# The opening of a second cross attention in a four-stage block: where the first queries, both query biases, the key blocks and two norms stand in their queues

## What is computed

```python
x = x + _L0_xattn_ref(_layernorm(x), ctx_768, ...)      # cross attention, 16 heads of 64
x = x + _L0_ffn_ref(_layernorm(x), ...)                 # shared MLP + top 2 of 8 experts
x = x + _L1_xattn_ref(_layernorm(x), ctx_768, ctx_768, ...)
x = x + _L1_ffn_ref(_layernorm(x), ...)                 # fp8 product with one scale over all of x
```

```python
Qp = query @ Wq + bq
K = _l2norm(key @ Wk + bk)
V = value @ Wv + bv
Q = _l2norm(Qp)
... # 16 heads of 16
scores = einsum('bhqd,bhkd->bhqk', Q, K) * SCALE
out = einsum('bhqk,bhkd->bhqd', softmax(scores), V)
x = out @ Wo + bo + Qp
... # then a layer norm with gamma and beta
```

## Time and profile before

| | |
|---|---|
| median of 3 runs | 931.23 us (927.85 to 932.57) |
| the profiled execution | 929.04 us, its span 927.0 us |
| PE busy | 859.7 us, 93% |
| PE weight load busy | 788.0 us, 85% |
| DVE busy | 723.2 us, 78% |
| ACT busy | 526.5 us, 57% |
| POOL busy | 361.9 us, 39% |
| mean granted TensorE clock | 0.961 of full speed |

### The profile page before, as it was taken

The page is one execution under the profiler, slowest core; times in us unless marked ns, Lnnn a source line. Parts: engine busy times, 40 slices in busy tenths (PEclk is TensorE's granted clock), DMA queues, the critical chain, the costliest instruction groups (busy, mean ns, idle before and its releaser), DMA issues. The chain is left out here.

```text
span 927.0 us, 18650 instructions
## 1 busy us (share of the span) xinstructions
PE 859.7 (93%) x5904; PEld 788.0 (85%) x5904; DVE 723.2 (78%) x1821; ACT 526.5 (57%) x1454; POOL 361.9 (39%) x412
## 2 busy tenths in 40 slices
PE   6899999999999999999979999999899999999435
PEld 6889999999999998899969999998688888888423
DVE  7788788978978978888756667877636889978988
ACT  5676566656756655454424445444436566665377
POOL 3133333423333424765631310243654757341330
PEclk9999999999999999999989999999879999999768
DMA  9999980000100003343324434544211111000003
GB/s 303 304 334 321 328 272 0 0 0 0 34 0 0 2 1 104 103 141 110 103 75 120 140 101 134 151 132 133 79 52 41 52 41 47 24 1 2 0 23 159
DMA packets 51771, 91.89 MB, mean 99 GB/s; under 512 B 5381, under 2 KB 26298, under 8 KB 51697
## 3 DMA queue, kind: packets, MB, share of 16 engines
q1 hardware_dynamic: 45105, 72.87, 24.7%
q0 software_dynamic: 6592, 18.07, 6.3%
HBM read 34.56 MB, written 56.36 MB: 98 GB/s over the span
## 5 line engine op out<-in xcount | busy, mean ns | idle before, releaser
L535 POOL TENSOR_TENSOR prob<-prob,row_inv 128x462 f32<-128x462 f32 (+1 forms) x96 | 83.6, 874 | 180.4 <-DVE row_inv L711 180.4
L898 PE MATMUL acc<-u,probT 128*128 128x256 f32 (+1 forms) x960 | 134.2, 289 | 1.0 <-DVE u L723 1.0
L595 ACT ACTIVATE prob<-score,neg_max 128x77 f32<-128x77 f32 x512 | 120.9, 351 | 14.6 <-DVE neg_max L705 14.3
L851 PE MATMUL score<-m,xnT 128*128 128x462 f32 (+1 forms) x576 | 124.2, 354 | 0.0
L898 PEld LDWEIGHTS acc<-u,probT 128*128 128x128 f32 (+1 forms) x960 | 119.5, 189 | 1.9 <-DVE u L723 1.4
L851 PEld LDWEIGHTS score<-m,xnT 128*128 128x128 f32 x576 | 97.6, 191 | 6.0
L1231 PE MATMUL py<-w1T,hidT 128*128 x426 | 93.5, 355 | 0.0
L2128 PEld LDWEIGHTS acc<-vz,prob 128*128 128x128 f32 (+1 forms) x640 | 80.2, 199 | 12.8 <-issue 11.2
L585 ACT ACTIVATE probT<-tr 128x512 fp32r<-128x512 f32 (+1 forms) x96 | 52.0, 544 | 66.3 <-PE tr L837 66.0
L1676 POOL DMA_INDIRECT dispatched<-xn,slots x64 | 69.2, 1082 | 43.9 <-DVEq L1460 26.6
L2128 PE MATMUL acc<-vz,prob 128*128 128x34 f32 (+2 forms) x640 | 82.4, 283 | 0.0
(11 more groups left out here) (381 smaller groups left out, 2086.7 us busy)
## 6 DMA issues: line engine op xcount, KB each, us to landing
dispatched<-zeros SPq DMA_DIRECT2D x1, 33664.0 KB, 111.0
xn<-dispatched SPq DMA_DIRECT2D x71, 128.0 KB, 2.0
dispatched<-hid SPq DMA_DIRECT2D x71, 128.0 KB, 1.7
out<-x_res SPq DMA_DIRECT2D x7, 512.0 KB, 2.6
x_res<-in_x SPq DMA_DIRECT2D x1, 3072.0 KB, 16.0
consts<-in_L_ffn_W SPq DMA_DIRECT2D x8, 384.0 KB, 3.4
consts<-in_L_ffn_Ws SPq DMA_DIRECT2D x3, 384.0 KB, 3.8
x_res<-in_x SPq DMA_DIRECT2D x2, 512.0 KB, 9.2
```

The lines of the kernel that those rows point to most:

```text
L535: gp.tensor_tensor(pr, pr, row_inv[t % 2][:, heads(k)].unsqueeze(2).to_broadcast([P, BANK_HEADS[k], KEYS]), ALU.mult).then_inc(prob_ready, 1)
L595: last = act.activation(prob[t % 2][:, h * KEYS:(h + 1) * KEYS], score_of(t, k)[:, n * KEYS:(n + 1) * KEYS], ACT.Exp, bias=neg_max[t % 2][ ...
L851: last = pe.matmul(score_of(t, k)[:, 0:BANK_HEADS[k] * KEYS], xnT[blk][i][:, dc, j * P:(j + 1) * P], m[w][:, dc, cols(k)], start=(n == 0 a ...
L898: last = pe.matmul(acc[t % 2][:, 0:D], probT[t % 2][i][0:rows, c, :], u[k][0:rows, c, :], start=(c == 0 and q == 0), stop=(c == KCH - 1 an ...
```

## The change

Four lists are written in another order; no instruction is added or taken away.

- PE and DVE: block 0's queries come behind two value rows instead of four, and DVE adds both biases one behind the other instead of with four value rows between them. The second half of the combine of block 1, its statistics, the low parts of block 0's queries and its shift are placed anew between the value rows. On PE two value rows (14 and 15) move behind the transposes of the queries.
- POOL: `gp_keys(0, 0)` comes behind the first gather of block 2, and `gp_ln(1)` behind two more gathers.
- ACT: the norm of block 1 stands in one piece behind the first two exponentials, where it had stood around them; the norm of block 2 comes before the copies of block 1's transposed queries, where it had stood behind them.

```diff
--- before.py
+++ after.py
@@ -2261,11 +2261,11 @@
             act_exp(act, 0, 8)
             act_unit_queries(act, 1)
             act_exp(act, 0, 9)
+            for a in range(2):
+                act_normalize(act, 2, a)
             act_split_q(act, 1, 0)
             act_turned(act, 0, 0)
             act_split_q(act, 1, 1)
-            for a in range(2):
-                act_normalize(act, 2, a)
             act_exp(act, 1, 0)
             act_exp(act, 1, 1)
             for dc in range(DC):
@@ -2602,13 +2602,14 @@
             @block.gpsimd
             def _(gp):
                 gp_gather(gp, 1, FIRST_PART)
-                gp_keys(gp, 0, 0)
                 for k in range(YT_BUFS):
                     gp.wait_ge(g["stored"][k], 16 * len(range(k, TILES_B, YT_BUFS)))
                 gp_gather(gp, 2, 0, 1)
+                gp_keys(gp, 0, 0)
                 gp_root(gp, 0)
+                gp_gather(gp, 2, 1, 3)
                 gp_ln(gp, 1)
-                gp_gather(gp, 2, 1, TJ)
+                gp_gather(gp, 2, 3, TJ)
                 gp_keys(gp, 0, 1)
                 gp_gather(gp, 2, TJ)
                 gp.memset(bias_rows[:, :], 0.0).then_inc(fs["rows_set"], 1)
@@ -2644,10 +2645,10 @@
                 act_unit_queries(act, 0)
                 for dc in range(DC):
                     act_split_q(act, 0, dc)
-                act_normalize(act, 1, 0)
                 act_exp(act, 0, 0)
                 act_exp(act, 0, 1)
-                act_normalize(act, 1, 1)
+                for a in range(2):
+                    act_normalize(act, 1, a)
                 act_first_block(act)
                 for n in range(1, NBLK):
                     act_block(act, n)
@@ -2714,17 +2715,18 @@
             def _(dve):
                 dve_combine(dve, 1, 0)
                 dve_row_sums(dve)
-                dve_value_rows(dve, range(0, 4))
-                dve_queries(dve, 0, 0)
-                dve_value_rows(dve, range(4, 8))
-                dve_queries(dve, 0, 1)
+                dve_value_rows(dve, range(0, 2))
+                for a in range(2):
+                    dve_queries(dve, 0, a)
+                dve_value_rows(dve, range(2, 6))
                 dve_combine(dve, 1, 1)
+                dve_value_rows(dve, range(6, 10))
                 dve_stats(dve, 1)
-                dve_value_rows(dve, range(8, 16))
-                dve_shift(dve, 1)
                 for dc in range(DC):
                     dve_split_q(dve, 0, dc)
-                dve_value_rows(dve, range(16, len(SPREAD)))
+                dve_value_rows(dve, range(10, 14))
+                dve_shift(dve, 1)
+                dve_value_rows(dve, range(14, len(SPREAD)))
                 dve_query_residual(dve, 0)
                 dve_first_block(dve)
                 for n in range(1, NBLK):
@@ -2809,12 +2811,13 @@
             def _(pe):
                 for dc in range(DC):
                     pe_transpose_x(pe, 0, dc)
-                pe_value_rows(pe, range(0, 4))
+                pe_value_rows(pe, range(0, 2))
                 for a in range(2):
                     pe_queries(pe, 0, a)
-                pe_value_rows(pe, range(4, 16))
+                pe_value_rows(pe, range(2, 14))
                 for dc in range(DC):
                     pe_transpose_q(pe, 0, dc)
+                pe_value_rows(pe, range(14, 16))
                 pe_scores(pe, 0, 0)
                 pe_value_rows(pe, range(16, len(SPREAD)))
                 pe_first_block(pe)
```

## The result

The changed kernel takes 929.49 us (median of 22 runs, 918.72 to 935.39) against 931.28 us of the kernel before (22 runs); the ratio is 0.9953, with a 95% interval of 0.9931 to 0.9974. That is 0.2 to 0.7% faster, at the edge of what this measurement tells from no change. The forecast was 919.5 us in a range of 915 to 927: it promised 11.8 us, and the medians differ by 1.8.

The account below looks back on a forecast made before the run. PE was taken as the bound, busy for 93% of the span, partly at half clock. Profiled 929.0 - 2.7 (scores) - 6.6 (clock) - 0.9 (norm) = 918.8 us; 919.5 forecast for the median, range 915 to 927.

Parts of the forecast that it names:

- Keys behind one gather: Block 0's first keys on POOL, moved clear of DVE's first combine: 3.03 us of DVE saved, 0 lost in the new place.
- The bound that I wrote down for it, 2.77 us: Most that POOL's first keys could cost DVE in their new time: the whole of the keys, 2.77 us.
- Queries behind two value rows: Block 0's opening: earlier queries and biases end PE's 1.80 us wait for qn; scores start 2.7 us earlier.
- The second keys: POOL's second key product would meet DVE's query residual or next combine, up to 2.8 us; 0 by block 1's slack.
- The clock: Block 0's 13.8 us half-clock stretch: PE idles only some 0.4 us ahead, clock stays at 2.4 GHz, -6.6 us.
- the clock falls all the same: Rival at block 0's first products, chance 0.22 with the long fall: 925.4 us, or up to 927.6.
- the 1.8 us: Block 0's clock: if every fall were as short as the first, the sum would lose only 1.8 us.
- Norm of block 2: ACT, end of block 0: norm goes into idle time ahead of the copies, PE's xn wait ends, -0.9 us; at worst 1.1 lost.
- Norm of block 1: ACT, behind block 0's first exponentials: one piece costs nothing, as two rounds of other work precede its transposes on PE.
- the chances of no change and of slower: Whole kernel: 0.18 for a time within 926.6 to 935.9 us, 0.03 for slower.

Follow-up runs that it names:

- The idle and filled runs: The repaired kernel with five more ACTIVATEs ahead of block 0's scaled queries, so PE idles: ratio 0.9965; the same with 16 identity transposes on PE then: 0.9917.
- the repaired kernel: Changed kernel with DVE's five row-sum copies ahead of block 1's first combine and block 1's shift ahead of four masks: ratio 0.984, 917.13 us.
- all three profiles on the last chip: Profiles of the repaired kernel run again (ratio 0.9833) and of its versions with PE idle (0.9965) and with the same delay filled (0.9917).
- the first four experiments: The first four follow-up runs, not listed by name, on a chip where the kernel before had a median of 932.7 us.

## Why the prediction was wrong

- *Keys behind one gather: 3.03 us of DVE saved, 0 in the new place.* This is the step that failed. The keys did start at 653.16, as worked out (653.2), and the combine took 1.67. I listed "the first two masks and a bias" as DVE's work in that time. By my own figures the copies ahead of the masks ran from 652.6 to 653.1, just ahead of the keys, and I named them as the only ones that the keys could touch, but gave that no term in the sum; the first of them began 0.55 us ahead of the keys and was held to their end, 3319 ns. A start ahead of them is no protection: the combine's instruction of 3507 ns had begun 0.5 us ahead too. The bound that I wrote down for it, 2.77 us, was if anything small: the copies took 3.1 us more. The Trainium skill ("SBUF — State Buffer", Who interferes with whom) has copies among the instructions that can take the shared port; the runs here agree, with 3.63 us beside the keys against 0.50 away from them.
- *Queries behind two value rows: scores 2.7 us earlier.* Scores began 15.2 us into the stage (664.29 less 649.07) against 17.1 before, 1.9 us; but the first transposes and value rows ran at full clock in this profile and at half before. Against the old order with full clock and DVE clear (15.4) it is 0.2, so by this edit next to nothing was had. The wait for qn stayed (2.06), as the last bias was late by what the copies were. With the copies out of the way it went to 0, as forecast, the scores began at 12.9, and DVE's masks didn't hold PE up ahead of them.
- *The second keys: 0, with slack.* I had them meet the residual or the combine. They met the shift, which is read by ACT's norm and followed by six masks: 3.00 us, of which PE saw 1.20.
- *The clock: -6.6 us.* The idle and filled runs support the mechanism, and the repaired kernel gives what the forecast wanted (0.984, some 15 us). Its condition, PE idle for some 0.4 us, wasn't met, so the clock fell in most runs: 0.962 against 0.976. The profile is one of those where it fell late and for 3.4 us, which is why it reads 922.6 where the median is 929.5. What I gave a chance of 0.22, "the clock falls all the same", is what happened, by way of the idle time that stayed. Its sum was 925.4 to 927.6 with the scores still 2.7 us earlier; without these my terms leave 929.0 - 0.9 = 928.1 for the profiled execution, near the median.
- *By the rule of the Trainium skill ("TensorE: Matmul & The Clock Gate", The HAM clock gate), that activity releases the throttle, every fall would be short.* It was 3.4 us here, and 17.0 and 22.9 in two other profiles with PE busy for 16.58 and 22.90 us of it: the measurements decide against the 1.8 us as a rule.
- *Norm of block 2: -0.9 us.* Right: the wait is gone, at either clock. *Norm of block 1: nothing.* Wrong in the term: with the shift held and the clock full, its old place left PE idle for 4.61 us. I looked at who waits for the norm, not at what stands behind it on ACT while it waits.
- Two sums were off by little: four of eight records of 3.71 us are 1.86 us and not 1.7, and the chances of no change and of slower add up to 0.19 and 0.02.

## What to carry to other kernels

When a transfer of work on GpSimd is moved off one VectorE instruction, look at every instruction of VectorE in the new time and a microsecond ahead of it, the smallest included: a copy of 16 columns was held as long as a combine of 256. Where TensorE is the bound, price a wait of two microseconds by what the clock does behind it and not by its length, and count the spread of the runs before relying on the clock of one profile. Where two things make an instruction late, freeing one leaves the other: here the scores came 2.3 us earlier only with both the queries' order and DVE's copies in their new places.

## What was not expected of the hardware

- A VectorE instruction already under way is held by GpSimd products that start half a microsecond later: 3319 and 3507 ns for instructions of some 0.1 and 0.48 us. A gather ran just ahead of the keys in both. A gather alone doesn't do it: the changed kernel's combine ran beside two of them (650.93 and 652.19) in 1.67 us. What a gather and the keys do together wasn't tested.
- The same idle time costs very different amounts: 2.06 us ahead of the transposes were followed by 3.4 us at half clock in one profile (a run of 922.6 us) and 17.0 in another, of the kernel with the shift moved. And PE idles for 1.40 or 1.41 us ahead of the stage's first transposes in all thirteen profiles: in five of them the stage opens at half clock, in eight at full. Idle time is not the whole of what decides.
- In all three profiles on the last chip PE stands idle ahead of the same scores (2.20, 2.40 and 2.46 us), behind an exponential that ACT started late, after idle time put down to "remote". In the two where the clock was full until then it fell. What ACT waited for stays open.
- The length of what comes ahead varies as well: in the profiles of the first four experiments, all on one chip, the second attention begins at 647.9 to 653.3 us. This part of the spread has nothing to do with the change and wasn't looked into.
